# A graph network's first two stages share one SBUF buffer, and the loop that sums edges is written out on two engines

## The chip, the cores and the metric

The kernel runs on one core of one Trainium2 chip. A core has five engines that work at the same time and meet through semaphores: TensorE (PE, matrix products into PSUM), VectorE (DVE), ScalarE (ACT), GpSimd (POOL) and SyncE (SP), which issues most transfers. The metric is device microseconds of one execution, the median of several runs. Everything is float32.

## The reference, cut to what matters

1250 nodes have 512 features each, and 40000 edges (`src`, `dst`, `edge_weight`) join them. The change touches the first half of this:

```python
deg = jnp.maximum(segment_sum(ones, dst), 1.0)
xn  = layernorm(x)
x   = x + gnn0(xn, src, dst, deg) + flow_attention(xn)   # gnn0: segment_sum(xn[src], dst)/deg @ W_neigh + xn @ W_self, normed
x   = x + experts0(layernorm(x))
xn  = layernorm(x)
x   = x + gnn1(xn, src, dst, edge_weight) + attention1(xn)   # gnn1 sums with edge weights
x   = x + experts1(layernorm(x))
```

Both sums over edges are products with a dense matrix: `counts[s, d]`, the number of edges from s to d, and `weights[s, d]`, the sum of their weights. The kernel builds both matrices once.

## The kernel before, in words

`program` runs five stages one after the other; a barrier of all engines stands between two of them.

**`flow_attention`** (0 to 600 us of the profile). The 1250 rows lie as `T` = 10 tiles of 125 rows by 512 features. In its first part the 40000 edges get places in a list that is sorted by groups of 32 destinations (`BUCKET`), and POOL writes the edge records to `sorted_edges` in HBM with 320 indirect DMAs (L310), one after the other. Beside that, PE, DVE and ACT compute the attention. DVE ends with `add_up` (L654), which adds the result to x in `g.x`. What is left then are the last tiles of `side(t)`: PE multiplies `xn` with the first graph layer's two matrices (L781, L784), ACT copies both products to a buffer that holds two tiles (L692), and SP stores them in HBM as `neighbour` and `own` (L512). ACT may overwrite its half of the buffer only when the stores of two tiles earlier have landed. After tile 6 SP also stores `g.x` itself as `x_spill` (L515), since its SBUF place is given up at the end of the stage.

**`adjacency`** (601 to 921 us) builds `counts` and `weights`, each 10 blocks of 1280 columns on 128 partitions, in a large buffer called `arena`. DVE first sets `counts` to zero (L923), POOL `weights` (L894). The sorted list has `NG` = 118 groups of 512 edges (4 chunks of 128). For each group:
- DVE makes 4 one-hot matrices of 128x320 of the destinations (L931) and the one-hot rows (128x128) of chunk 3 of the sources (L933);
- POOL copies three columns of numbers (L901) and makes the one-hot rows of chunks 0 to 2 (L909), then, one group behind, `row_low` of chunk 3 (L914);
- ACT scales the rows by both halves of the weight, 7 operations (L964, L966);
- PE multiplies: 4 matmuls into `ps_c`, 8 into `ps_w` (L982 to L987), at full width 320;
- DVE, two groups behind, adds `ps_c` to the 10x32 columns of `counts` and `ps_w` to those of `weights` (L944). Which 32 columns is read from a table on chip into a register.

All five engines run this as loops over registers, four groups a turn (`staggered`), with 4 buffers (`BUFS`). So group t can begin when the product of group t-4 is done (semaphore `used`).

**`nodes`** (921 us on) reads `x_spill` back into `x_rows` (L1162), sums degrees, and combines. On DVE the sum of a tile is made in `h`, which holds `own` (loaded in the stage before, L889); POOL adds a row of biases to x (L1206). The last two stages are the experts and the gathering of their results.

## Time and profile before

| | us |
|---|---|
| median of 3 runs | 2133.72 |
| lowest and highest of them | 2128.21, 2137.45 |
| the profiled execution | 2126.98 |
| its span, first to last instruction | 2125.2 |
| adjacency: first one-hot of DVE to last addition of a product | 614.34 to 918.76 |

The page of the profile gives each engine's busy time over the whole span: PE 81%, DVE 43%, ACT 24%, POOL 41%. These are means over stages that differ; within `adjacency` all four are busy for most of the time. The rows further down are in us from the span's start. In a row of the timeline the first number is the start and the second the time from there to the end of the last instruction that it merges; the time from one start to the next is the step that the engine needs. "idle before <-" names what ended an engine's idle time.

### The profile page before, as it was taken

How to read it: one execution, taken by the hardware profiler on the slowest of the kernel's cores; microseconds unless marked ns; L12 is line 12 of the kernel's file. 1: busy time of each engine (PE TensorE's matmuls, PEld its weight loads, DVE VectorE, ACT ScalarE, POOL GpSimd, SP SyncE). 2: the span in 40 equal slices, each digit the busy share in tenths (PEclk: the TensorE clock that was granted, in tenths of full speed). 3: DMA queues.
4: the chain of work that ended last, by engine and by line, in shares of the span. 5: the costliest groups of instructions: out<-in, count | busy, mean ns of one | idle time of the engine just before them, and what ended most of it. 6: DMA issues, size and time to landing. Idle time of an engine off the chain costs nothing. (4 is left out here: it accounts for less than half of the span.)

```text
span 2125.2 us, 27922 instructions
## 1 busy us (share of the span) xinstructions
PE 1715.3 (81%) x8075; PEld 1126.1 (53%) x8076; DVE 919.6 (43%) x2223; ACT 519.3 (24%) x1459; POOL 875.1 (41%) x1032
## 2 busy tenths in 40 slices
PE   4649988756937777786879999279999999999992
PEld 4224434334436666652434465157777777777770
DVE  3852266344159999969845638400000000000001
ACT  0011101111138888820111122011222211122220
POOL 0677778777669999965011100220000000043002
PEclk9999998978969999998889999589999999999996
DMA  7900031000230000010210013543803320420003
GB/s 202 298 2 2 2 76 31 2 2 2 65 114 25 0 0 0 0 61 0 94 56 1 0 37 122 211 131 150 331 20 144 150 76 20 178 63 20 20 20 102
DMA packets 77073, 150.32 MB, mean 71 GB/s; under 512 B 19795, under 2 KB 21402, under 8 KB 72802
## 3 DMA queue, kind: packets, MB, share of 16 engines
q1 hardware_dynamic: 50533, 125.26, 16.5%
q0 software_dynamic: 19200, 11.30, 3.7%
q10 hardware_dynamic: 7294, 13.21, 1.8%
q8 instruction: 23, 0.38, 0.1%
q14 instruction: 23, 0.18, 0.0%
HBM read 111.35 MB, written 37.99 MB: 70 GB/s over the span
## 5 line engine op out<-in xcount | busy, mean ns | idle before, releaser
L310 POOL DMA_INDIRECT sorted_edges<-fa_records,fa_edge_slot x320 | 399.4, 1248 | 176.2 <-issue 176.2
L1838 PEld LDWEIGHTS et_ps_h<-et_turned,arena 128*128 128x128 f32 x3072 | 348.6, 193 | 19.2 <-issue 15.9
L1838 PE MATMUL et_ps_h<-et_turned,arena 128*128 128x128 f32 x3072 | 349.1, 276 | 7.6 <-issue 4.5
L1847 PE MATMUL et_ps_y<-arena,et_hidden_t 128*128 x768 | 333.6, 592 | 0.0
L909 POOL TENSOR_SCALAR ad_row<-iota,ad_row_no 128x128 fp32r<-128x128 f32 x354 | 237.9, 685 | 0.1
L1847 PEld LDWEIGHTS et_ps_y<-arena,et_hidden_t 128*128 128x128 f32 x768 | 144.0, 190 | 172.2 <-issue 172.2
L1749 POOL DMA_INDIRECT xn_rows<-slot_out,slots x10 | 12.2, 1218 | 493.8 <-POOLq L1746 491.0
L986 PE MATMUL ad_ps_w<-ad_to,ad_row_high 128*128 128x320 f32 x472 | 150.1, 330 | 63.5 <-POOL ad_row_low L914 60.5
L964 ACT ACTIVATE ad_row_high<-ad_row,ad_edges 128x128 fp32r<-128x128 f32 x472 | 184.5, 391 | 67.9 <-DVE ad_row L933 67.0
L1765 DVE COPY et_turned<-et_ps_t 128x512 f32<-128x512 f32 x25 | 17.3, 692 | 370.7 <-PE et_ps_t L1819 370.7
L931 DVE TENSOR_SCALAR ad_to<-iota,ad_edges 128x320 fp32r<-128x320 f32 x472 | 176.6, 433 | 0.0
L1775 DVE TENSOR_TENSOR et_y<-et_ps_y,et_b 128x512 f32<-128x512 f32 x24 | 16.6, 691 | 318.1 <-PE et_ps_y L1847 318.1
L1795 ACT ACTIVATE et_hidden_t<-et_ps_h,ex_b 128x128 f32<-128x128 f32 x384 | 109.7, 369 | 143.9 <-PE et_ps_h L1838 141.2
L987 PE MATMUL ad_ps_w<-ad_to,ad_row_low 128*128 128x320 f32 x472 | 140.9, 310 | 0.0
L986 PEld LDWEIGHTS ad_ps_w<-ad_to,ad_row_high 128*128 128x128 f32 x472 | 89.4, 189 | 90.9 <-ACT ad_row_high L964 90.9
L966 ACT ACTIVATE ad_row_low<-ad_row,ad_edges 128x128 fp32r<-128x128 f32 x354 | 137.3, 388 | 0.0
L1795 ACT ACT_TABLE_LOAD x24 | 30.8, 1283 | 434.2 <-PE et_ps_h L1838 434.2
L1604 PE MATMUL no_banks<-arena,no_turned 128*125 128x512 f32 (+1 forms) x320 | 114.4, 515 | 7.1 <-ACT no_turned L1231 7.1
L1537 PE MATMUL no_banks<-xn_rows,arena 125*125 125x512 f32 x200 | 97.6, 648 | 21.3 <-DVE arena L1320 17.6
L982 PE MATMUL ad_ps_c<-ad_to,ad_row 128*128 128x320 f32 x472 | 89.6, 312 | 31.3 <-DVE ad_row L933 31.3
L739 PE MATMUL fa_banks<-ident,fa_work 125*128 125x125 f32 x120 | 23.3, 329 | 103.1 <-DVE fa_work L551 45.3
L1216 POOL TENSOR_TENSOR x_rows<-x_rows,no_normed 125x512 f32<-125x512 f32 x10 | 12.7, 1271 | 208.4 <-DVE no_normed L1379 208.4
(363 smaller groups left out, 2327.2 us busy)
## 6 DMA issues: line engine op xcount, KB each, us to landing
arena<-L_ffn_W SPq DMA_DIRECT2D x16, 4096.0 KB, 13.3
slot_rows<-fa_zeros SPq DMA_DIRECT2D x1, 7424.0 KB
slot_out<-fa_zeros SPq DMA_DIRECT2D x1, 6912.0 KB
et_rows_in<-slot_rows ACTq DMA_DIRECT2D x26, 256.0 KB, 2.6
slot_out<-et_y ACTq DMA_DIRECT2D x24, 256.0 KB, 2.0
sorted_edges<-fa_records,fa_edge_slot POOLq DMA_INDIRECT x320
x_in<-x SPq DMA_DIRECT2D x1, 2500.0 KB
neighbour<-fa_Wv SPq DMA_DIRECT2D x10, 250.0 KB
```

Of the source, the lines that this page charges most:

```text
L310: nc.gpsimd.indirect_dma_start(g.sorted_edges, bass.IndirectOffsetOnAxis(ap=self.edge_slot[0:NT, e:e + 1], axis=0), self.records[0:NT, e, ...
L909: last = nc.gpsimd.tensor_scalar(row[:, u, c, :], g.iota[:, 0:P], row_no[:, u, c:c + 1], None, ALU.is_equal)
L931: v.tensor_scalar(to[:, u, c, :], g.iota[:], field(t, c, 1), None, ALU.is_equal)
L964: last = nc.scalar.activation(row_high[:, u, c, :], row[:, u, c, :].bitcast(F32), ACT.Copy, scale=field(t, c, 2))
L966: nc.scalar.activation(row_low[:, u, c, :], row[:, u, c, :].bitcast(F32), ACT.Copy, scale=field(t, c, 3))
L986: pe.matmul(ps_w[:, u, 0:ONE_HOT], row_high[:, u, c, :], to[:, u, c, :], start=(c == 0), stop=False)
L987: last = pe.matmul(ps_w[:, u, 0:ONE_HOT], row_low[:, u, c, :], to[:, u, c, :], start=False, stop=(c == CHUNKS - 1))
L1537: last = pe.matmul(banks[r, t % 3, :], counts[r, b, t * NT:(t + 1) * NT], g.xn[r, b, :], start=(b == 0), stop=(b == T - 1))
L1604: last = pe.matmul(banks[r, bank, 0:GCN] if name == "conv" else banks[r, bank, :], turned[:, t % 2, k * NT:(k + 1) * NT], matrix[:, k, :], ...
L1795: last = nc.scalar.activation(hidden_t[:, f * KD + i, :], ps_h[:, f % 2, i, :], ACT.Gelu, bias=x.b1[:, bass.ds(e * FT + (f * KD + i), 1)])
L1838: last = pe.matmul(ps_h[:, f % 2, i, :], x.weights[:, at:at + P], turned[:, k, :], start=(k == 0), stop=(k == KD - 1))
L1847: last = pe.matmul(ps_y[:], hidden_t[:, i, :], x.weights[:, bass.ds(buffer * (2 * HALF) + (HALF + i * D), D)], start=(i == 0), stop=(i == ...
```

## The change

It does five things.

1. **x stays on chip.** `arena` (32768 float32 a partition) is made at the very start. `g.x` in the first stage is its part behind `weights` and `counts`, which now lie side by side at its front. The first stage's big buffers (q, k, v, work, Wo, W1, W2 and others) are cut out of that front. `x_spill`, its store and its load are gone.
2. **The zeroing moves.** DVE clears both matrices (25600 elements a partition) in one memset at the end of the first stage, behind `add_up`. Both memsets of `adjacency` are gone.
3. **`own`** is loaded at the start of `nodes` into `x_rows`, where `x_spill` was loaded, and not during `adjacency`. In `nodes` the buffers `h` and `g.x` change their roles.
4. **The loops of DVE and POOL are written out** for all 118 groups, so that addresses are constants; only the columns of the addition stay in a register. ACT and PE keep their loops. POOL's copy of the numbers is gone. POOL makes 3 rows in even groups and 2 in odd ones; DVE makes 1 and 2. POOL's `row_low` runs two groups behind, where it ran one behind.
5. **One addition a group**: `ps_w` and `ps_c` are halves of one PSUM tensor, and one DVE instruction adds 2x10x32 columns to both matrices.

```diff
-                if t == SIDE[1]:
-                    sp.wait_ge(s["x_final"], 1)
-                    sp.dma_start(g.x_spill.rearrange("(t p) d -> p t d", p=NT), g.x[0:NT]).then_inc(s["x_stored"], 16)
-            sp.wait_ge(s["x_stored"], 16)
...
             staggered(c, 8, prepare_ff, nothing, add_up)
             c.settle()
-            dve.sem_inc(s["x_final"], 1)
+            c.link(v.memset(arena[:, 0:2 * T * DST], 0.0))
...
-        ps_c, ps_w = m.psum("ps_c", [P, BUFS, 512]), m.psum("ps_w", [P, BUFS, 512])
+        ps = m.psum("ps", [P, BUFS, 2, 512])
+        ps_w, ps_c = ps[:, :, 0, :], ps[:, :, 1, :]
+        totals = arena[:, 0:2 * T * DST].rearrange("p (m b n) -> p m b n", m=2, b=T)
...
+        def pool_rows(t):
+            return 3 - t % 2
...
-            sp.dma_start(own_rows[0:NT], g.own.rearrange("(t p) d -> p t d", p=NT)).then_inc(arrived, 16)
...
-            nc.gpsimd.memset(weights, 0.0).then_inc(zeroed, 1)
...
-                for c in range(POOL_ROWS):
-                    last = nc.gpsimd.tensor_scalar(row[:, u, c, :], g.iota[:, 0:P], row_no[:, u, c:c + 1], None, ALU.is_equal)
+                for c in range(pool_rows(t)):
+                    last = nc.gpsimd.tensor_scalar(row[:, u, c, :], g.iota[:, 0:P], field(t, c, 0), None, ALU.is_equal)
...
-            staggered(Steps(pool, chain), 0, fetch_numbers, build_rows, scale_low, NG, BUFS)
+            in_turn(build_rows, scale_low, NG, BUFS)
...
-                for ps, total in ((ps_c, counts), (ps_w, weights)):
-                    part = total[:, :, bass.ds(at, BUCKET)]
-                    last = v.tensor_tensor(part, part, ps[:, u, 0:ONE_HOT].rearrange("p (b n) -> p b n", b=T), ALU.add)
+                part = totals[:, :, :, bass.ds(at, BUCKET)]
+                v.tensor_tensor(part, part, ps[:, u, :, 0:ONE_HOT].rearrange("p m (b n) -> p m b n", b=T), ALU.add).then_inc(added, 1)
...
-            sp.dma_start(g.x[0:NT], g.x_spill.rearrange("(t p) d -> p t d", p=NT)).then_inc(s["x_in"], 16)
+            sp.dma_start(g.x[0:NT], g.own.rearrange("(t p) d -> p t d", p=NT)).then_inc(s["own_in"], 16)
```

`in_turn(first, third, n, ways)` is a plain loop that calls `first(t)` and then `third(t - 2)`, for t from 0 to n + 1.

What that does to an engine's row of instructions is seen at three places. On DVE, the end of one group in the middle of `adjacency` (ISA and REGISTER_ALU rows compute addresses in registers, and one ISA row stands ahead of each of the four one-hots) before:

```order
L931 TENSOR_SCALAR ad_to<-iota,ad_edges 128x320
L933 ISA
L933 TENSOR_SCALAR ad_row<-iota,ad_edges 128x128
L937 ISA
L937 TENSOR_LOAD group_offset
L937 ISA x2
L939 REGISTER_ALU
L941 REGISTER_ALU [waits ad_used]
L944 ISA [waits ad_added]
L944 TENSOR_TENSOR arena<-arena,ad_ps_c 128x10x32
L944 ISA
L944 TENSOR_TENSOR arena<-arena,ad_ps_w 128x10x32
```

And a whole group of DVE at the same place after the change, an odd one:

```order
L947 TENSOR_SCALAR ad_to<-iota,ad_edges 128x320 [waits ad_used]
L947 TENSOR_SCALAR ad_to<-iota,ad_edges 128x320 x3
L949 TENSOR_SCALAR ad_row<-iota,ad_edges 128x128 x2
L953 TENSOR_LOAD group_offset
L953 ISA x2
L959 ISA [waits ad_added,ad_used]
L959 TENSOR_TENSOR arena<-arena,ad_ps 128x20x32
```

The address steps between the one-hots are gone, the two additions are one of twice the size, and every second group has a second row. On POOL, one group in the same place before:

```order
L901 COPY ad_row_no<-ad_edges 128x3
L909 TENSOR_SCALAR ad_row<-iota,ad_row_no 128x128 [waits ad_used,ad_numbered]
L909 TENSOR_SCALAR ad_row<-iota,ad_row_no 128x128 x2
L914 ISA [waits ad_columns_made]
L914 TENSOR_TENSOR ad_row_low<-ad_row,ad_edges 128x128
```

And two groups of POOL after the change:

```order
L929 TENSOR_SCALAR ad_row<-iota,ad_edges 128x128 [waits ad_used]
L929 TENSOR_SCALAR ad_row<-iota,ad_edges 128x128 x2
L934 TENSOR_TENSOR ad_row_low<-ad_row,ad_edges 128x128 [waits ad_columns_made]
L929 TENSOR_SCALAR ad_row<-iota,ad_edges 128x128 [waits ad_used]
L929 TENSOR_SCALAR ad_row<-iota,ad_edges 128x128
L934 TENSOR_TENSOR ad_row_low<-ad_row,ad_edges 128x128 [waits ad_columns_made]
```

The copy is gone, and five rows stand where six stood. On DVE at the passage from the first stage to `adjacency`, before:

```order
L654 TENSOR_TENSOR x_in<-x_in,fa_work 125x512 [waits fa_f_out]
L448 UNCONDITIONAL_BRANCH [waits fa_chain]
L920 UNCONDITIONAL_BRANCH [waits barrier_Pool_Activation_PE_DVE_SP_release]
L923 MEMSET arena 128x12800
L931 TENSOR_SCALAR ad_to<-iota,ad_edges 128x320 [waits ad_loaded,ad_used,ad_zeroed,ad_chain]
```

And the same passage after:

```order
L680 TENSOR_TENSOR arena<-arena 125x512 [waits fa_f_out]
L684 MEMSET arena 128x25600 [waits fa_chain]
L474 UNCONDITIONAL_BRANCH [waits fa_chain]
L939 UNCONDITIONAL_BRANCH [waits barrier_Pool_Activation_PE_DVE_SP_release]
L947 TENSOR_SCALAR ad_to<-iota,ad_edges 128x320 [waits ad_used,ad_loaded]
```

The memset has moved to the other side of the barrier and doubled.

## Rows read from the trace of the kernel before

**Rows 1.** Busy time by stretch: engines with counts, granted clock, DMA share, GB/s

```profile
614.30:921.40 307.10, 237.95 (x1417) 210.32 (x1417) 302.18 (x838) 254.92 (x826) 299.91 (x585) 0.98 0.04 14
```

**Rows 2.** Timeline, end of the first stage: start, us, engine, line, instruction [idle before]

```profile
546.58 0.69 DVE L654 TENSOR_TENSOR x_in<-x_in,fa_work 125x512 f32<-125x512 f32 x1
...
555.97 0.34 SPq L515 DMA_DIRECT2D x_spill<-x_in  x1
...
577.65 7.75 SPq L512 DMA_DIRECT2D own<-fa_Wv  x1
...
579.26 1.19 POOL L310 DMA_INDIRECT sorted_edges<-fa_records,fa_edge_slot  x1 [0.30 <-issue]
...
583.87 1.12 PE L784 MATMUL fa_banks<-fa_bq,ones 1*125 1x512 f32 x2
592.38 1.07 ACT L692 COPY fa_Wv<-fa_banks 125x512 f32<-125x512 f32 x2 [17.32 <-DMA own<-fa_Wv]
...
593.48 0.25 SPq L512 DMA_DIRECT2D own<-fa_Wv  x1
```

**Rows 3.** Timeline, start of adjacency, SP and DVE

```profile
600.85 0.35 SPq L886 DMA_DIRECT2D ad_edges<-sorted_edges  x1
...
603.58 10.72 DVE L923 MEMSET arena<- 128x12800 f32 x1 [56.32 <-issue]
605.45 0.27 SPq L888 DMA_DIRECT2D xn_rows<-neighbour  x1
...
614.34 1.57 DVE L931 TENSOR_SCALAR ad_to<-iota,ad_edges 128x320 fp32r<-128x320 f32 x4
```

**Rows 4.** Timeline of DVE near the program's start, POOL idle

```profile
11.54 0.33 DVE L327 MEMSET fa_turned<- 128x320 f32 x1
11.88 0.33 DVE L328 MEMSET fa_turned<- 40x320 f32 x1
...
12.30 0.31 DVE L331 CAST fa_high_r<-fa_work 125x320 fp32r<-125x320 f32 x1
12.53 0.32 DVE L332 CAST fa_turned<-fa_work 125x320 f32<-125x320 int32 x1
...
13.41 0.76 DVE L335 TENSOR_TENSOR fa_records<-fa_work,fa_high_r 125x320 f32<-125x320 f32 x1
```

**Rows 5.** Timeline, one group in the loop's steady part: DVE, POOL and ACT

```profile
903.89 2.01 POOL L909 TENSOR_SCALAR ad_row<-iota,ad_row_no 128x128 fp32r<-128x128 f32 x3
...
904.57 1.50 DVE L931 TENSOR_SCALAR ad_to<-iota,ad_edges 128x320 fp32r<-128x320 f32 x4
...
905.87 0.46 POOL L914 TENSOR_TENSOR ad_row_low<-ad_row,ad_edges 128x128 fp32r<-128x128 f32 x1
...
905.99 0.41 DVE L933 TENSOR_SCALAR ad_row<-iota,ad_edges 128x128 fp32r<-128x128 f32 x1
...
906.33 0.47 DVE L944 TENSOR_TENSOR arena<-arena,ad_ps_c 128x320 f32 x1
...
906.43 2.01 POOL L909 TENSOR_SCALAR ad_row<-iota,ad_row_no 128x128 fp32r<-128x128 f32 x3
...
906.50 0.40 ACT L964 ACTIVATE ad_row_high<-ad_row,ad_edges 128x128 fp32r<-128x128 f32 x1 [0.28 <-DVE ad_row L933]
...
906.72 0.47 DVE L944 TENSOR_TENSOR arena<-arena,ad_ps_w 128x320 f32 x1
```

**Rows 6.** Timeline of DVE where the groups already have constant addresses: first and last

```profile
617.61 0.30 DVE L933 TENSOR_SCALAR ad_row<-iota,ad_edges 128x128 fp32r<-128x128 f32 x1
617.81 1.43 DVE L931 TENSOR_SCALAR ad_to<-iota,ad_edges 128x320 fp32r<-128x320 f32 x4
...
912.22 1.42 DVE L931 TENSOR_SCALAR ad_to<-iota,ad_edges 128x320 fp32r<-128x320 f32 x4
913.57 0.41 DVE L933 TENSOR_SCALAR ad_row<-iota,ad_edges 128x128 fp32r<-128x128 f32 x1
```

**Rows 7.** Timeline, start of nodes, POOL

```profile
946.73 13.18 POOL L1206 TENSOR_TENSOR x_rows<-x_rows,arena 125x512 f32<-125x512 f32 x10 [10.40 <-DMA no_gate_b<-L_ffn_bg]
```

More of the change, by code:

```diff
@@ L123, in staggered, with in_turn @@
     third(n - 1, (n - 1) % ways)
+def in_turn(first, third, n, ways):
+    for t in range(n + 2):
+        if t < n:
+            first(t, t % ways)
+        if t >= 2:
+            third(t - 2, (t - 2) % ways)
 def nothing(t, u):
@@ L853, in _, with adjacency @@
                 side(t)
-def adjacency(nc, g, counts, weights, own_rows):
+def adjacency(nc, g, arena):
     BUFS = 4
-    POOL_ROWS = 3
     POOL_LOW = 1
@@ L922, in _ @@
             v = nc.vector
-            v.memset(counts, 0.0).then_inc(chain, 1)
-            dve.wait_ge(chain, 1)
-            dve.wait_ge(zeroed, 1)
             dve.wait_ge(loaded, 16)
@@ L931, in build_columns @@
                     v.tensor_scalar(to[:, u, c, :], g.iota[:], field(t, c, 1), None, ALU.is_equal)
-                for c in range(POOL_ROWS, CHUNKS):
+                for c in range(pool_rows(t), CHUNKS):
                     last = v.tensor_scalar(row[:, u, c, :], g.iota[:, 0:P], field(t, c, 0), None, ALU.is_equal)
@@ L941, in add @@
                 dve.wait_ge(added, t + BUFS)
-                for ps, total in ((ps_c, counts), (ps_w, weights)):
-                    part = total[:, :, bass.ds(at, BUCKET)]
-                    last = v.tensor_tensor(part, part, ps[:, u, 0:ONE_HOT].rearrange("p (b n) -> p b n", b=T), ALU.add)
-                last.then_inc(added, 1)
-            staggered(Steps(dve, chain), 0, build_columns, nothing, add, NG, BUFS)
+                part = totals[:, :, :, bass.ds(at, BUCKET)]
+                v.tensor_tensor(part, part, ps[:, u, :, 0:ONE_HOT].rearrange("p m (b n) -> p m b n", b=T), ALU.add).then_inc(added, 1)
+            in_turn(build_columns, add, NG, BUFS)
             dve.wait_ge(added, NG + BUFS)
@@ L953, in _ @@
             last.then_inc(chain, 1)
-            dve.wait_ge(chain, 2)
+            dve.wait_ge(chain, 1)
         @block.scalar
@@ L1885, in program @@
         g = Shared(nc, stack)
-        with ExitStack() as first:
-            g.x = Memory(nc, first).sb("x_in", [P, T, D])
-            flow_attention(nc, A, g)
+        arena = Memory(nc, stack).sb("arena", [P, 2 * 2 * HALF])
+        weights, counts = (arena[:, i * T * DST:(i + 1) * T * DST].rearrange("p (t n) -> p t n", t=T) for i in range(2))
+        rows = arena[:, 2 * T * DST:2 * T * DST + T * D].rearrange("p (t d) -> p t d", t=T)
+        g.x = rows
+        flow_attention(nc, A, g, arena)
         with ExitStack() as layer:
-            arena = Memory(nc, layer).sb("arena", [P, 2 * 2 * HALF])
             x = Experts(nc, A, layer, arena)
-            weights, counts = (arena[:, i:i + T * DST].rearrange("p (t n) -> p t n", t=T) for i in (0, T * DST + T * D))
-            h = arena[:, T * DST:T * DST + T * D].rearrange("p (t d) -> p t d", t=T)
-            adjacency(nc, g, counts, weights, h)
+            adjacency(nc, g, arena)
             g.x = Memory(nc, layer).sb("x_rows", [P, T, D])
-            nodes(nc, A, g, x, arena, weights, counts, h)
+            nodes(nc, A, g, x, arena, weights, counts, rows)
             expert_tiles(nc, A, g, x)
```

72 lines of the change are left out of this document (40 added, 32 removed).

## The prediction

> **What bounds the kernel now.** I read the busy time by stretch first, then the timeline of the two places that the diff touches. In `adjacency` (307.10 us) DVE is busy for 302.18 us and POOL for 299.91, ACT for 254.92, PE for 237.95, and PE's granted clock is 0.98, the level of 2.4 GHz [rows 1]. So two engines have no slack there. The steady part shows it: POOL starts its three rows at 903.89 and again at 906.43, so a group takes 2.54 us; DVE's one-hots start at 904.57, its row at 905.99, its additions at 906.33 and 906.72, each right behind the one before, while ACT waits 0.28 us for DVE's row [rows 5]. 118 groups at 2.55 are 301 of the 304.4 us between first one-hot and last addition.
>
> At the passage into `adjacency` other things end last. PE's last product of the first stage ends at 584.99 (583.87 + 1.12). ACT copies it only from 592.38, after 17.32 us of idle time that a store of `own` ended; that store stood in SP's queue behind the 2.5 MB of `x_spill`, issued at 555.97, and its issue alone took 7.75 us [rows 2]. The last store goes out at 593.48 [rows 2], and the edge list is asked for at 600.85, behind the barrier [rows 3]. It is there at 605.45, where SP goes on, but DVE makes its first one-hot at 614.34, since its memset comes first [rows 3].
>
> **The change part by part.**
>
> *x is not stored.* Without the spill the stores of tile 7 go out when they are made, and ACT's wait goes. Next late is PE's last product, at 584.99, then a copy of 0.6, so the last store goes out at about 585.7, which is 7.8 earlier than 593.48. Before, it had a second store 0.5 us ahead of it, and both and the barrier took 7.4 us (593.48 to 600.85). After, that other store is over 4 us ahead. So 7.4 is the upper bound and 4.7, somewhat over half, the lower; I take 5.2, nearer the lower, as only one store is left to wait for. The edge list is then asked for at 590.9, 10 us earlier (bounds 7.8 and 10.5). POOL's last indirect DMA was issued at 579.26 [rows 2]; nothing makes it later, and 11 us are left for it to land.
>
> *The memset moves.* DVE's memset of 320 elements takes 0.335 us from start to start (11.54 to 11.88) [rows 4], 1.04 ns an element. 12800 elements are 13.4 us: DVE was free from the barrier at about 600.9 and went on at 614.3, so the row's 10.72 shows only its later part [rows 3]. 25600 elements take 26.8 us. DVE's last addition ends at 547.3 [rows 2], so it is done at 574.1, covered by the stage's end at 590, with 16 us to spare. If that cover were gone it would cost what lies over 590. In `adjacency` DVE then waits for the edge list alone: 614.34 - 605.45 = 8.9 us less, sure within 0.3.
>
> The Trainium skill (SBUF — State Buffer, "SBUF: two separate sides") warns that VectorE work which takes both ports keeps GpSimd from writing the descriptors of its DMAs, and POOL still has such DMAs to issue when the new memset runs. The same skill (VectorE: DVE Perf Modes, "Zero memsets can be issued as uint32") gives a memset one cycle an element, and the 1.04 ns above agree, so I take it for no such work; the other case is a rival.
>
> *`own` is loaded later.* It takes the place of the load of `x_spill`, of the same 2.5 MB, as first transfer of `nodes`. POOL's wait there was ended by the small `gate_b` behind it in the queue [rows 7], and that stays. DVE needs both too. 0 us.
>
> *The loop, for one group.* DVE is the engine to sum, in steps from start to start:
> - four one-hots: 1.42 in the loop (904.57 to 905.99) [rows 5], 1.35 with constant addresses (912.22 to 913.57) [rows 6]: -0.07.
> - half a row more: 0.20 where another comparison follows (617.61 to 617.81) [rows 6], 0.34 ahead of an addition [rows 5]: +0.10, at worst +0.17.
> - the additions: 0.39 and 0.40 before (906.33 to 906.72, and on to the next group). The second now lacks its start and costs its elements alone, 320 at 1.04 ns [rows 4]: 0.40 + 0.33 = 0.73, so -0.06. Bounds: 0 if nothing is saved; the slow form is a rival.
> - what DVE and POOL cost each other. A one-hot takes 0.34 while POOL works; a cast of the same 320 elements takes 0.23 with POOL idle (12.30 to 12.53) [rows 4]. With the row (0.34 against 0.20) that is 4 x 0.11 + 0.14 = 0.58 us a group that POOL's presence costs. POOL was busy for 98% [rows 1]. After, it makes 2.5 rows at 0.66 (three took 903.89 to 905.87) and one `row_low` of 0.46 [rows 5], 2.1 us of 2.4: idle for a seventh. A seventh of 0.58 is 0.08; were all of the 0.3 us idle under one-hots, it would be 0.3 x 0.58 / 1.69 = 0.10. I take -0.09. The bounds are 0 and -0.58.
>
> Sum: -0.12 us, 2.43 a group; times 118, 14 us. ACT's 254.92 / 118 = 2.16 us a group [rows 1] lies below that and PE's 2.02 too, so both keep their slack. POOL's copy was free of DVE and goes with it. `row_low` is a group later: it follows the rows of group t+2, which follow the product of t-2, and two groups at 2.43 are 4.86 us against about 2.0 + 0.5 for POOL and 1.3 for the product. It hides. That code written out comes slower to an engine is not seen in any row; 0.
>
> **Sum**: 10 + 8.9 + 14 = 33 us. The profiled execution took 2126.98 us, below the lowest of the three runs, so its own figure would be 2094; against the median of 2133.72 it is 2101, which I forecast.
>
> **The rivals.**
>
> *POOL's slack frees DVE altogether.* If the 0.58 us go for the most part, ACT's loop becomes the bound at 2.16 a group: (2.55 - 2.16) x 118 = 46, and 2133.7 - 19 - 46 = 2069. For it speaks that both engines run in lock-step now, without a gap; against it that POOL stays busy for over four fifths. The Trainium skill (SBUF — State Buffer, "Who interferes with whom") says that the two engines' shared ports are an exclusive lock, held for a whole instruction, and the loser fully blocks. By that rule half a row of 0.6 and the copy of 0.18 would come off the shared time, 0.48 us a group or 57 in all, near 2058. The rows disagree so far: DVE makes four one-hots and a row from 904.57 to 906.33 while POOL makes three rows from 903.89 to 905.87 [rows 5]; in turn they would need more than 2.54 us.
>
> *Nothing comes off the loop.* POOL's idle time falls under DVE's additions, where it helps nobody, and the extra half row eats the rest: 2.50 to 2.58 a group, and 2133.7 - 19 with -6 to +4: 2109 to 2119.
>
> *The memset stops POOL's DMAs*, the skill's warning. Then 26.8 us are added to POOL's chain, 580.5 + 26.8 = 607 and a landing, some 10 us behind 600.85 and not 10 ahead of it: 2101 + 20 = 2121. Against it: 1.04 ns an element.
>
> *The wide addition is slow*, the one that ends slower. An addition with strided operands took 0.76 us for 320 elements, at 13.41 [rows 4], where L944 takes 0.47 [rows 5]. Should 2x10x32 columns fall to that, it takes 1.5 us, not 0.73: +0.79 a group, +93 us, near 2194. From a step of 1.10 us on the kernel gets slower than before by 0.5%. Against it: the parts before had the same runs of 32 and did not pay for them.
>
> **How the numbers follow.** Forecast (2092 to 2109) 0.50; POOL's slack frees DVE (2058 to 2092) 0.25; nothing off the loop 0.15; memset stops POOL 0.05; slow addition 0.05. A measurement of this kernel can tell about 0.5%, 10.7 us, from no change. Below 2123 lie the first three and most of the fourth: faster 0.90, same 0.05, slower 0.05. The range runs from 2066, which leaves out a part of the second case, to 2119.
>
> **What would show it.** The edge list asked for near 591 and the first one-hot 4.6 us behind it; no wait of ACT on `own`; the memset between 547 and 574, POOL's 1.5 us rhythm of indirect DMAs unbroken beside it. In the loop: period near 2.43; the addition's step 0.73; one-hots 0.31 to 0.34; ACT waiting for DVE about 0.2 us a group, POOL idle for 0.3. A period of 2.16 with ACT never idle is the first rival, one-hots still at 0.34 with POOL idle the second. I am wrong altogether if the addition's step is over 1.1 us or POOL's DMAs stop from 547 on.

## The result, and the profile after

The changed kernel takes 2096.31 us (median of 4 runs, 2095.41 to 2099.82), the kernel before 2130.97 in the same comparison (4 runs, 2123.45 to 2137.45). The ratio is 0.984, with a 95% interval of 0.981 to 0.988. The forecast was 2101, 4.7 us above, with a range of 2066 to 2119. The profiled execution took 2099.82 us (span 2098.0), the one of before 2126.98.

First the busy times of the changed kernel by stretch: the first stage up to VectorE's last addition, the passage up to the first one-hot, the edge sum, and the rest in three. The columns after the stretch are its length and each engine's busy us.

```profile
core 0: us, PE busy (x) PEld busy (x) DVE busy (x) ACT busy (x) POOL busy (x), PEclk, DMA share, GB/s
0.00:544.90 544.90, 382.69 (x1353) 198.70 (x1355) 268.33 (x475) 56.87 (x104) 378.72 (x312) 0.94 0.26 60
544.90:593.10 48.20, 35.72 (x84) 14.36 (x82) 21.43 (x2) 6.39 (x11) 25.23 (x22) 0.87 0.27 65
593.10:887.30 294.20, 241.11 (x1416) 210.27 (x1416) 287.90 (x767) 254.57 (x826) 257.15 (x413) 0.98 0.02 9
887.30:1036.80 149.50, 116.58 (x364) 57.26 (x364) 119.45 (x313) 14.64 (x22) 53.59 (x28) 0.87 0.16 55
1036.80:1387.40 350.60, 272.02 (x1056) 159.71 (x1057) 179.60 (x551) 50.88 (x103) 52.32 (x40) 0.87 0.22 79
1387.40:2098.00 710.60, 668.40 (x3805) 484.38 (x3803) 40.70 (x58) 135.56 (x395) 52.81 (x40) 0.97 0.28 99
```

The stretches of before were 547.3, 67.0, 304.5, 148.9, 346.8 and 710.7 us long. Side by side, with the last three put together:

| stretch | before | after | difference |
|---|---|---|---|
| first stage | 547.3 | 544.9 | -2.4 |
| VectorE's last addition there to first one-hot | 67.1 | 48.2 | -18.9 |
| first one-hot to end of last edge addition | 304.4 | 294.3 | -10.1 |
| from there to the end | 1206.4 | 1210.6 | +4.2 |

The change shows in the second and third line, 29.0 us together. The other two lines hold its quieter parts (x in `arena`, `own` loaded in `nodes`), and they differ between executions of one kernel too. From the last addition to the end of TensorE's last product in `nodes` it is 433.5 us before, 434.9 in this profile, 436.7 in a second profile of the changed kernel (after_again) and 433.5 in store_x, a variant that loads `own` at the same place: that load costs nothing that can be seen. The whole part behind the edge sum takes 1207.3 to 1214.5 us in the profiles of the changed kernel and its variants and 1206.4 in the single one of before. Whether a few us of that are a cost of the change is not shown.

The passage, in the changed kernel's timeline of VectorE, SyncE's queue and ScalarE (start, duration, what runs, idle time before it and its releaser):

```profile
544.21 0.69 DVE L680 TENSOR_TENSOR arena<-arena 125x512 f32<-125x512 f32 x1
550.29 21.39 DVE L684 MEMSET arena<- 128x25600 f32 x1 [5.40 <-issue]
...
582.65 0.59 ACT L718 COPY fa_Wv<-fa_banks 125x512 f32<-125x512 f32 x1 [3.84 <-PE fa_banks L810]
...
583.26 0.25 SPq L542 DMA_DIRECT2D own<-fa_Wv  x1
587.62 0.35 SPq L916 DMA_DIRECT2D ad_edges<-sorted_edges  x1
```

ScalarE's last copy waits for its product only, where the one of before waited 17.32 us for a store of `own` [rows 2]. The edge list is asked for 42.7 us after VectorE's last addition; before it was 53.6 (600.85 less 547.27) [rows 3]. From asking to the first one-hot it is 5.4 us, where it was 13.5. These two steps are 10.9 and 8.0 us.

The start of the loop, on GpSimd, TensorE and VectorE:

```profile
593.12 5.81 POOL L929 TENSOR_SCALAR ad_row<-iota,ad_edges 128x128 fp32r<-128x128 f32 x8 [13.21 <-DMA ad_edges<-sorted_edges]
598.90 0.40 POOL L934 TENSOR_TENSOR ad_row_low<-ad_row,ad_edges 128x128 fp32r<-128x128 f32 x1
...
599.45 0.61 PE L1000 MATMUL ad_ps<-ad_to,ad_row_high 128*128 128x320 f32 x1 [2.36 <-POOL ad_row_low L934]
...
593.06 1.52 DVE L947 TENSOR_SCALAR ad_to<-iota,ad_edges 128x320 fp32r<-128x320 f32 x4 [21.37 <-DMA ad_edges<-sorted_edges]
...
602.07 0.82 DVE L959 TENSOR_TENSOR arena<-arena,ad_ps 128x640 f32 x1 [3.87 <-PE ad_ps L1001]
```

The first addition comes 9.0 us after the first one-hot; before it was 6.85. TensorE waits 2.36 us for `row_low` of group 0, which stands behind eight rows on GpSimd. No term of the prediction had this.

The steady part, VectorE, then GpSimd, then ScalarE:

```profile
751.37 0.81 DVE L959 TENSOR_TENSOR arena<-arena,ad_ps 128x640 f32 x1
752.10 1.36 DVE L947 TENSOR_SCALAR ad_to<-iota,ad_edges 128x320 fp32r<-128x320 f32 x4
753.39 0.30 DVE L949 TENSOR_SCALAR ad_row<-iota,ad_edges 128x128 fp32r<-128x128 f32 x1
753.58 0.81 DVE L959 TENSOR_TENSOR arena<-arena,ad_ps 128x640 f32 x1
...
751.96 0.40 POOL L934 TENSOR_TENSOR ad_row_low<-ad_row,ad_edges 128x128 fp32r<-128x128 f32 x1
752.72 2.14 POOL L929 TENSOR_SCALAR ad_row<-iota,ad_edges 128x128 fp32r<-128x128 f32 x3 [0.35 <-PE ad_ps L1001]
754.82 0.46 POOL L934 TENSOR_TENSOR ad_row_low<-ad_row,ad_edges 128x128 fp32r<-128x128 f32 x1
...
751.70 0.40 ACT L978 ACTIVATE ad_row_high<-ad_row,ad_edges 128x128 fp32r<-128x128 f32 x1 [0.57 <-DVE ad_row L949]
```

VectorE runs without a gap: the addition's step is 0.73 us (751.37 to 752.10), a group with one row on VectorE takes 2.21. The next one, with two, takes about 2.65. The 21st addition starts at 650.95 and the 111th at 870.57, 2.440 us a group; before these were 671.68 and 901.22, 2.550. GpSimd now waits 0.35 us for the product; it had no idle time in [rows 5].

### The profile page after: what moved, and what is told of

Read it like the earlier page. It is cut to its first block and busy times, and to the rows that moved or that the text cites. A ratio compares the mean times of both kernels' runs of the same rounds, so it can differ in the third digit from the quotient of the medians.

```text
span 2098.0 us, 26207 instructions
## 1 busy us (share of the span) xinstructions
PE 1716.5 (82%) x8075; PEld 1124.7 (54%) x8076; DVE 917.4 (44%) x2164; ACT 518.9 (25%) x1459; POOL 819.8 (39%) x854
## 5 line engine op out<-in xcount | busy, mean ns | idle before, releaser
L929 POOL TENSOR_SCALAR ad_row<-iota,ad_edges 128x128 fp32r<-128x128 f32 x295 | 210.8, 727 | 42.8 <-PE ad_ps L1001 29.6
L1000 PE MATMUL ad_ps<-ad_to,ad_row_high 128*128 128x320 f32 x472 | 153.2, 337 | 49.6 <-ACT ad_row_high L978 46.8
L947 DVE TENSOR_SCALAR ad_to<-iota,ad_edges 128x320 fp32r<-128x320 f32 x472 | 168.3, 415 | 21.4 <-DMA ad_edges<-sorted_edges 21.4
L1001 PE MATMUL ad_ps<-ad_to,ad_row_low 128*128 128x320 f32 x472 | 140.9, 310 | 0.0
L1000 PEld LDWEIGHTS ad_ps<-ad_to,ad_row_high 128*128 128x128 f32 x472 | 89.4, 189 | 80.2 <-ACT ad_row_high L978 77.5
L765 PE MATMUL fa_banks<-ident,arena 125*128 125x125 f32 x120 | 22.6, 321 | 102.9 <-DVE arena L577 45.4
L996 PE MATMUL ad_ps<-ad_to,ad_row 128*128 128x320 f32 x472 | 89.6, 312 | 13.1 <-POOL ad_row L929 13.1
L959 DVE TENSOR_TENSOR arena<-arena,ad_ps 128x640 f32 x118 | 95.3, 807 | 6.3 <-PE ad_ps L1001 6.2
```

What stands on the lines that cost most here:

```text
L929: last = nc.gpsimd.tensor_scalar(row[:, u, c, :], g.iota[:, 0:P], field(t, c, 0), None, ALU.is_equal)
L947: v.tensor_scalar(to[:, u, c, :], g.iota[:], field(t, c, 1), None, ALU.is_equal)
L959: v.tensor_tensor(part, part, ps[:, u, :, 0:ONE_HOT].rearrange("p m (b n) -> p m b n", b=T), ALU.add).then_inc(added, 1)
L1000: pe.matmul(ps_w[:, u, 0:ONE_HOT], row_high[:, u, c, :], to[:, u, c, :], start=(c == 0), stop=False)
L1001: last = pe.matmul(ps_w[:, u, 0:ONE_HOT], row_low[:, u, c, :], to[:, u, c, :], start=False, stop=(c == CHUNKS - 1))
```

## The experiments

All are the changed kernel with the edit named; after_again has none. The table has the numbers of each profile on which the verdicts rest: **passage** is from VectorE's last addition of the first stage to the first one-hot, **start** from there to the first edge addition, **period** from the 21st to the 111th addition divided by 90, **sum** from the first one-hot to the end of the last addition, all in us. The median is of all its timed executions; pool_idle, whose results are wrong, has a single one.

| kernel | passage | start | period | sum | median |
|---|---|---|---|---|---|
| before | 67.1 | 6.85 | 2.550 | 304.4 | 2130.97 |
| changed kernel | 48.2 | 9.0 | 2.440 | 294.3 | 2096.31 |
| after_again | 48.2 | 9.0 | 2.431 | 293.3 | 2094.87 |
| store_x | 57.9 | 9.0 | 2.429 | 293.6 | 2112.74 |
| clear_in_adjacency | 56.2 | 6.9 | 2.429 | 291.4 | 2107.81 |
| low_early | 46.4 | 7.4 | 2.431 | 291.7 | 2093.13 |
| two_adds | 48.0 | 9.0 | 2.418 | 292.2 | 2094.09 |
| dve_rolled | 48.2 | 9.0 | 2.425 | 293.0 | 2095.81 |
| pool3 | 49.3 | 9.6 | 2.410 | 291.3 | 2091.94 |
| pool_idle | 48.3 | 9.0 | 2.218 | 269.3 | 2076.14 |
| dve_as_before | 48.1 | 9.6 | 2.486 | 300.4 | 2105.39 |
| pool_as_before | 47.9 | 8.1 | 2.617 | 314.0 | 2115.19 |
| best | 47.9 | 7.7 | 2.392 | 287.6 | 2091.28 |
| best2 | 48.0 | 7.7 | 2.419 | 291.0 | 2098.88 |

The kernel before, timed beside the later ones, had medians of 2124.6 to 2126.3. The medians carry some us that no edit explains, so sizes of single edits are read from the stretches of each kernel's one profile.

**The measure.**

> The changed kernel itself once more, as the measure for the other runs beside it: period of a group 2.43 to 2.44, first addition 9.0 us after the first one-hot, 294 us from the first one-hot to the end of the last addition, 48 us from VectorE's last addition of the first stage to the first one-hot. What differs between its profile and the first one (outside adjacency above all) is what one profiled execution can't tell.

It held. The period differs by 0.009 and the sum by 1.0 us from the first profile, in which three groups took 0.22 us longer than their like. The part behind the edge sum took 1209.2 us, 1.4 less than in the first profile. How far one passage can be trusted is seen in low_early and pool3, which edit nothing there: 46.4 and 49.3 us. From asking for the edge list to the first one-hot it is 5.2 to 5.5 us in every run that leaves it alone.

### The passage

**The store of x, put back.**

> The changed kernel, with x stored to the spill buffer again between the stores of neighbour and own, and waited for at the end of the stage (nothing reads it). Theory: the store of own queues behind it and ScalarE's last copies wait, so the edge list is asked for 10 to 11 us later, 53 to 54 us after VectorE's last addition of the first stage where it was 42.7; adjacency itself unchanged; the total 10 to 11 us more. Rival: in the kernel before the delay came from GpSimd's scatter or the barrier, and the store costs under 5 us. The clear of the totals, now at the same time, is not touched.

```
+                if t == SIDE[1]:
+                    sp.wait_ge(s["x_final"], 1)
+                    sp.dma_start(g.x_spill..., g.x[0:NT]).then_inc(s["x_stored"], 16)
+            sp.wait_ge(s["x_stored"], 16)
```

SyncE's queue and ScalarE of this kernel:

```profile
550.79 0.36 SPq L546 DMA_DIRECT2D x_spill<-arena  x1
555.50 13.12 SPq L543 DMA_DIRECT2D neighbour<-fa_Wv  x1
...
587.37 0.25 SPq L543 DMA_DIRECT2D own<-fa_Wv  x1
594.81 0.35 SPq L922 DMA_DIRECT2D ad_edges<-sorted_edges  x1
...
586.27 1.07 ACT L724 COPY fa_Wv<-fa_banks 125x512 f32<-125x512 f32 x2 [16.38 <-DMA own<-fa_Wv]
```

The pattern of before is back: an issue that takes 13.12 us behind the big store, ScalarE 16.38 us without work until a store of `own` has landed. The edge list is asked for 52.7 us after the first stage's last addition (594.81 less 542.10) and not 42.7. The cost is 9.8 us in the passage and nothing elsewhere; the rival (under 5 us) falls. Of the delay, 3.1 us lie behind the last store: 7.44 us from it to the asking, against 4.36 without the big store in the queue.

**The clear, put back into adjacency.**

> The changed kernel, with the totals cleared where the kernel before did it: at the start of adjacency, half by VectorE and half by GpSimd. Theory: from the asking for the edge list to the first one-hot 13.5 us instead of 5.44, so 8.05 later. GpSimd's half ends about 2 us before VectorE's, so GpSimd gets a lead and the first addition comes 7 to 7.5 us after the first one-hot instead of 9.01: 6 us more in all up to the last addition. Rival 1: no lead, 8 us more. Rival 2: the clear beside the first stage was not free and its removal there gives something back (GpSimd's last indirect DMA or the last store of own earlier by over 1 us): under 5 us more.

```
-            c.link(v.memset(arena[:, 0:2 * T * DST], 0.0))
+            nc.gpsimd.memset(arena[:, 0:T * DST], 0.0).then_inc(zeroed, 1)      # GpSimd, adjacency
+            v.memset(arena[:, T * DST:2 * T * DST], 0.0).then_inc(chain, 1)     # VectorE, adjacency
```

Timeline of SyncE, VectorE and GpSimd:

```profile
592.53 0.35 SPq L915 DMA_DIRECT2D ad_edges<-sorted_edges  x1
...
595.27 10.72 DVE L942 MEMSET arena<- 128x12800 f32 x1 [45.46 <-issue]
606.03 1.62 DVE L950 TENSOR_SCALAR ad_to<-iota,ad_edges 128x320 fp32r<-128x320 f32 x4
...
592.98 10.76 POOL L922 MEMSET arena<- 128x12800 f32 x1 [13.17 <-POOLq L474]
603.73 5.11 POOL L929 TENSOR_SCALAR ad_row<-iota,ad_edges 128x128 fp32r<-128x128 f32 x8
```

From asking to the first one-hot it is 13.50 us, as forecast. GpSimd starts 2.3 us ahead of VectorE, and the start takes 6.9 us instead of 9.0. So the clear costs 8.1 us and gives back 2.1 at the start, with `row_low` as late as in the changed kernel; passage and sum together are 5.1 us longer than in the first profile of the changed kernel and 6.1 longer than in the second. That is the theory (6 us, by way of the lead); 8 falls, and so does a gain of over 3 us elsewhere. GpSimd's last indirect DMA starts 28.8 us after the first stage's last addition (578.63 less 549.81), against 33.8 and 30.3 in the two profiles of the changed kernel, but the edge list waits for the last store of `own` (588.17), not for it.

**What the medians say of these two.** store_x is 17.9 us slower than after_again, clear_in_adjacency 12.9: 8 and 7 us more than in the stretches. TensorE's mean granted clock goes with it: 0.938 to 0.942 in the four executions of after_again, 0.934 to 0.938 in the six of store_x, 0.933 to 0.939 in the four of clear_in_adjacency. Executions of one kernel differ like that too: of the nine of the kernel before that were timed beside after_again, one took 2136.11 us at 0.933, one 2123.26 at 0.938 and one 2120.39 at 0.936. So a lower clock goes with a longer time, but not strictly; that it makes these 7 to 8 us is likely and not shown, and why these two kernels are granted less is open. The granted clock in the passage, 0.79 before and 0.87 after, is part of the mean and too little of it: by an estimate from these figures, 10 us more at 0.79 move the mean over 2100 us by 0.001.

**row_low earlier.**

> The changed kernel, with GpSimd's row_low of a group made one group after its rows instead of two (as in the kernel before). Start theory: the changed kernel loses about 2 us at the start of adjacency, because row_low of group 0 stands behind eight rows on GpSimd and the first addition comes 9.01 us after the first one-hot, where it was 6.85. With the shorter lag it stands behind five rows: the first addition 6.8 to 7.2 us after the first one-hot, the steady period 2.43 as before, the total 2 us less. Rival: the lag matters in the steady part, GpSimd waits for VectorE's row in every group, and the period rises to 2.48 or more, the total by 4 us or more. Second rival: what ends the start is TensorE or ScalarE, the first addition stays at 9.0.

```
-            in_turn(build_rows, scale_low, NG, BUFS)
+            in_turn(build_rows, scale_low, NG, BUFS, 1)     # third(t - 1), not third(t - 2)
```

Start of the loop on GpSimd, TensorE and VectorE:

```profile
588.88 3.86 POOL L929 TENSOR_SCALAR ad_row<-iota,ad_edges 128x128 fp32r<-128x128 f32 x5 [11.71 <-DMA ad_edges<-sorted_edges]
592.71 0.46 POOL L934 TENSOR_TENSOR ad_row_low<-ad_row,ad_edges 128x128 fp32r<-128x128 f32 x1
...
593.59 0.63 PE L1000 MATMUL ad_ps<-ad_to,ad_row_high 128*128 128x320 f32 x1 [0.74 <-ACT ad_row_high L978]
...
596.23 0.82 DVE L959 TENSOR_TENSOR arena<-arena,ad_ps 128x640 f32 x1 [2.25 <-PE ad_ps L1001]
```

`row_low` now follows five rows, TensorE waits for ScalarE and not for it, and the start is 7.4 us. The start theory holds in kind (1.6 us of the 2.2 that were lost, a little less than the 1.8 to 2.2 expected). It isn't the only cause: the start is 6.9 us in clear_in_adjacency, where `row_low` stayed late and GpSimd had its lead back. So the 2.2 us are lost where the later `row_low` and the lost lead come together; in the steady part the lag changes nothing, 2.431 in both.

### The loop

**Two additions again.**

> The changed kernel, with two additions of 128x320 a group instead of one of 128x640. Theory of the prediction, VectorE's steps add up: the additions take 0.79 to 0.82 a group instead of 0.73 to 0.71, the period goes from 2.43 to 2.49 to 2.53, 7 to 12 us more. Rival, VectorE's step is covered by the wait for the product or given back by GpSimd's free time: period 2.43 to 2.45, up to 2 us more.

```
-                part = totals[:, :, :, bass.ds(at, BUCKET)]
-                v.tensor_tensor(part, part, ps[:, u, :, 0:ONE_HOT]..., ALU.add).then_inc(added, 1)
+                for m_ in (1, 0):
+                    part = totals[:, m_, :, bass.ds(at, BUCKET)]
+                    last = v.tensor_tensor(part, part, ps[:, u, m_, 0:ONE_HOT]..., ALU.add)
```

The two take 0.79 us a group (752.50 to 753.29) instead of 0.73, as the prediction priced them, and yet the period falls from 2.431 to 2.418. Groups of instructions of this kernel in the edge sum (busy us, mean ns of one, idle time before):

```profile
L947 DVE TENSOR_SCALAR ad_to<-iota,ad_edges 128x320 fp32r<-128x320 f32 x472 | 161.4, 401 | 21.2 <-DMA ad_edges<-sorted_edges 21.2
...
L960 DVE TENSOR_TENSOR arena<-arena,ad_ps 128x320 f32 x236 | 103.0, 475 | 6.1 <-PE ad_ps L1003 6.1
```

A one-hot's row has a mean of 401 ns here and 415 in the changed kernel, so four of them give back about 0.06 us. The theory (2.49 to 2.53) falls. The period even lies a little under the rival's 2.43 to 2.45: the wide addition is worth nothing in this loop.

**VectorE's addresses in registers again.**

> The changed kernel, with VectorE's work in adjacency in a loop with register addresses again, four groups a round; GpSimd's stays written out, the split of the rows and the wide addition stay. Theory of the prediction: a one-hot through a register costs 0.07 a group more (1.42 against 1.35 for four), the period goes from 2.43 to 2.50, 8 us more. Rival: what made the one-hots shorter is GpSimd's freer time and not the addresses, the period stays within 0.01 of 2.43. Second rival: with GpSimd less loaded the loop's own branch and register work shows, 2.55 or more.

```
-            in_turn(build_columns, add, NG, BUFS)
+            staggered(Steps(dve, chain), 0, build_columns, nothing, add, NG, BUFS)
```

The period is 2.425, the one-hots' mean 412 ns. The first rival holds in its number: the constant addresses on VectorE are worth nothing here. The shorter one-hots of [rows 6], on which the prediction rested this term, lie in the last group. GpSimd was busy beside them, but without its copy of the row numbers; its rows in the kernel before:

```profile
908.82 0.18 POOL L901 COPY ad_row_no<-ad_edges 128x3 f32<-128x3 f32 x1
...
910.96 0.46 POOL L914 TENSOR_TENSOR ad_row_low<-ad_row,ad_edges 128x128 fp32r<-128x128 f32 x1
911.40 2.06 POOL L909 TENSOR_SCALAR ad_row<-iota,ad_row_no 128x128 fp32r<-128x128 f32 x3
```

The one-hots of 912.22 to 913.57 fall under the last three rows (911.40 to 913.46) and the `row_low` behind them. In pool3, next, which has three rows and no copy on GpSimd throughout, four one-hots take 1.35 us as well (751.62 to 752.96).

**Three rows on GpSimd.**

> The changed kernel, with GpSimd making three rows in every group (as in the kernel before) and VectorE one. Theory A, both engines limit: GpSimd needs three rows of about 0.66 us and a row_low of 0.46 without its copy, a period of 2.36 to 2.40, 4 to 8 us less than the changed kernel. Theory B, VectorE alone limits and GpSimd has room: its groups with one row take 2.21 already, so the period is 2.21 and the time 25 us less. Theory C, the split was worth its place, GpSimd and VectorE slow each other more with GpSimd always busy: the period is 2.43 to 2.48 and nothing is won or some us are lost.

The edit is `return 3` for `return 3 - t % 2`. Period 2.410: theory A, just above its range of 2.36 to 2.40, and B and C fall. Both engines run without a gap (of 280.8 us from the first addition to the last, VectorE is busy 278.5 and GpSimd 275.6). The half row that the change moved to VectorE, together with GpSimd's relief, costs 0.02 a group; the start is 0.6 us longer with three rows a group, which leaves 2.0 us less in the sum.

**GpSimd nearly without work.**

> The changed kernel, with GpSimd's operations on rows and row_low cut to 2 of 128 columns from the fifth group on (so the weights and counts of these groups are wrong); number and order of all instructions and waits stay. Theory: GpSimd's presence costs VectorE time. Its one-hots go to 0.295 and its rows to 0.2, a group to 2.11 with one row and 2.31 with two, 2.21 on the mean, unless ScalarE or TensorE take over at 2.16: period 2.16 to 2.25, 21 to 32 us less. Rival: VectorE's steps don't depend on GpSimd, period 2.40 to 2.44.

```
-                    last = nc.gpsimd.tensor_scalar(row[:, u, c, :], g.iota[:, 0:P], ...)
+                    n = P if t < BUFS else 2
+                    last = nc.gpsimd.tensor_scalar(row[:, u, c, 0:n], g.iota[:, 0:n], ...)
```

VectorE's timeline, and under it its groups in the edge sum:

```profile
750.97 0.81 DVE L961 TENSOR_TENSOR arena<-arena,ad_ps 128x640 f32 x1
751.70 1.27 DVE L949 TENSOR_SCALAR ad_to<-iota,ad_edges 128x320 fp32r<-128x320 f32 x4
752.89 0.50 DVE L951 TENSOR_SCALAR ad_row<-iota,ad_edges 128x128 fp32r<-128x128 f32 x2
753.29 0.81 DVE L961 TENSOR_TENSOR arena<-arena,ad_ps 128x640 f32 x1
```

```profile
L949 DVE TENSOR_SCALAR ad_to<-iota,ad_edges 128x320 fp32r<-128x320 f32 x472 | 149.7, 375 | 21.5 <-DMA ad_edges<-sorted_edges 21.5
...
L961 DVE TENSOR_TENSOR arena<-arena,ad_ps 128x640 f32 x118 | 95.3, 807 | 6.4 <-PE ad_ps L1003 6.4
```

The theory holds. GpSimd is still busy for 124.8 of 269.3 us, so VectorE is not quite alone. Four one-hots take 1.19 us (751.70 to 752.89), a group 2.11 with one row and 2.32 with two. So of 2.43 in the changed kernel 2.22 are VectorE's own and 0.21 come from GpSimd's presence. The addition is 807 ns here and 807 in the changed kernel, where a one-hot is 375 here and 415 there: GpSimd slows the one-hots and leaves the addition alone.

So three parts of the loop's change are worth nothing each, or next to it, when undone alone. That leaves GpSimd's code: the copy of the row numbers is gone and its loop is written out. The next two kernels put each side of the loop as it was.

**VectorE's side as before.**

> The changed kernel, with VectorE's part of the loop as in the kernel before (a loop with register addresses, one row a group, two additions of 128x320) and GpSimd's written out with constant addresses, three rows a group and no copy. Theory, formed after the first eight runs: the period of 2.55 was GpSimd's own (copy, three rows, row_low), and what the change brought in the loop is the copy that is gone; VectorE's changes are worth nothing, because a shorter step of VectorE only moves its one-hots under more of GpSimd's work. Then the period is 2.40 to 2.43 here. Rival: VectorE's changes count when all three are undone at once (0.07 for addresses, 0.10 for the addition), 2.48 to 2.55.

Period 2.486, with 0.79 for the additions. The theory falls and the rival holds, at the low end of its range. GpSimd's new code, with three rows still, brings 0.064 of the 0.11 to 0.12 (2.550 to 2.486). How much of that is the copy, and how much the written-out loop, no run separates. VectorE's register addresses and two additions together cost 0.076 against pool3, although beside two and a half rows on GpSimd each alone costs nothing. The edge sum fits: 300.4 us.

**GpSimd's side as before.**

> The changed kernel, with GpSimd's part of the loop as in the kernel before (a loop, a copy of three row numbers for each group, three rows, row_low one group after the rows) and VectorE's written out with constant addresses, one row a group and the wide addition. Theory: GpSimd alone sets the period, 2.53 to 2.57 as in the kernel before, although VectorE has everything that the change gave it. Rival: VectorE's shorter additions count, 2.43 to 2.48. The first addition comes 7.5 to 8.5 us after the first one-hot, since row_low is early again.

Timeline of VectorE and GpSimd, and under it the group of the one-hots:

```profile
751.87 0.81 DVE L969 TENSOR_TENSOR arena<-arena,ad_ps 128x640 f32 x1
752.60 1.66 DVE L957 TENSOR_SCALAR ad_to<-iota,ad_edges 128x320 fp32r<-128x320 f32 x4
754.19 0.38 DVE L959 TENSOR_SCALAR ad_row<-iota,ad_edges 128x128 fp32r<-128x128 f32 x1
754.49 0.81 DVE L969 TENSOR_TENSOR arena<-arena,ad_ps 128x640 f32 x1
...
752.66 0.39 POOL L943 TENSOR_TENSOR ad_row_low<-ad_row,ad_edges 128x128 fp32r<-128x128 f32 x1
753.00 0.28 POOL L930 COPY ad_row_no<-ad_edges 128x3 f32 x1
753.26 2.04 POOL L938 TENSOR_SCALAR ad_row<-iota,ad_row_no 128x128 fp32r<-128x128 f32 x3
```

```profile
L957 DVE TENSOR_SCALAR ad_to<-iota,ad_edges 128x320 fp32r<-128x320 f32 x472 | 195.4, 473 | 21.1 <-DMA ad_edges<-sorted_edges 21.1
```

Period 2.617, above both ranges and above the kernel before, which has the same work on GpSimd and more on VectorE. Four one-hots take 1.59 us here (752.60 to 754.19), 1.42 before [rows 5]. With the shorter addition and constant addresses on VectorE the loop is slower by 0.07. That GpSimd alone sets the period is false too: the same GpSimd code runs at 2.55 and at 2.62, without a gap in both. Its instructions themselves take other times: the copy 0.18 before (908.82, above) and 0.28 here (753.00).

### A kernel faster than both

**best.**

> The changed kernel with GpSimd making three rows in every group, row_low of a group one group after its rows, and ScalarE making the fourth row_low in every second group (eight scalings of 0.294 us there instead of seven), so that GpSimd's row_low runs in half the groups. Theory: VectorE alone needs 2.11 a group with one row, GpSimd busy for 2.0 to 2.2 costs it 0.25 to 0.27: period 2.36 to 2.38 where it is 2.43, and the first addition 1.5 to 3 us earlier; 8 to 11 us less than the changed kernel. Rival: ScalarE, 2.36 in the groups with eight scalings and no slack left, becomes the bound, the period is 2.43 or more. Second rival: GpSimd was no longer what slows VectorE, the period stays at 2.41 as with three rows alone.

```
-            return 3 - t % 2
+            return 3
...
+                if t % 2 == 0:
+                    return                       # GpSimd: no row_low in every second group
...
-            in_turn(build_rows, scale_low, NG, BUFS)
+            in_turn(build_rows, scale_low, NG, BUFS, 1)
...
-                    if c < CHUNKS - POOL_LOW:
+                    if c < CHUNKS - POOL_LOW * (u % 2):      # ScalarE: eight scalings there
```

Period 2.392, a little above the theory's 2.36 to 2.38; the sum is 287.6 us, 5.7 less than after_again, and not the 8 to 11 expected. low_early's earlier `row_low` and pool3's rows alone make 1.6 and 2.0 of that. The engines in the edge sum:

```profile
589.70:877.40 287.70, 240.42 (x1416) 209.55 (x1416) 282.19 (x709) 266.31 (x885) 268.51 (x413) 0.99 0.03 9
```

Its ratio to the kernel before is 0.985 (0.983 to 0.987), that of the changed kernel 0.984 and 0.983 in two comparisons. In the stretch the gain is plain; in the whole time, 2091.28 against 2096.31 and 2094.87, it is smaller than the intervals.

**best2.**

> As the run best (row_low one group after the rows; ScalarE makes the fourth row_low in every second group), but GpSimd makes three rows in the groups where ScalarE takes row_low and two in the others, VectorE one and two. VectorE alone needs 2.21 a group on the mean; GpSimd is busy for about 1.65 of it, less than in any run so far. Theory, the less GpSimd does the less VectorE is held up: period 2.30 to 2.36, first addition 7 to 7.5 us after the first one-hot, 281 to 284 us from the first one-hot to the end of the last addition where best took 287.6 and the changed kernel 293.3. Rival: the cost depends on which instruction of one engine lies beside which of the other more than on how much GpSimd does, and the period is anywhere from 2.36 to 2.42. Second rival: ScalarE with eight scalings (2.36) in every second group holds those groups, and the mean is 2.36 or more.

The theory missed: 2.419, although GpSimd is busy for only 226.1 of 291.1 us, less than in best (268.5 of 287.7). The groups alternate between 2.40 and 2.43. The first rival holds by its range, and the second (ScalarE) isn't excluded by this run, since ScalarE is busy for 269.0 of the 291.1 us.

## Why the prediction was right, and where it was not

**The passage was right in mechanism and size.** The store of x: 10 forecast, 10.9 between the two kernels, 9.8 when it alone is put back. The prediction's 5.2 us from the last store to the edge list (bounds 4.7 to 7.4) measured 4.36, a little below its lower bound. The clear: 8.9 forecast, 8.0 measured, 8.1 when put back; the term lost 0.8 because the edge list takes 5.4 us from asking to the first one-hot and not 4.6. Sum 19 against 18.9. The clear ran from behind the last addition (544.90) to its end at 571.68, 26.8 us, inside the time that TensorE's last products take, as forecast. GpSimd's indirect DMAs kept their 1.49 us steps beside it but for one pause of 3.69 us; before, with no clear there, one pause was 6.33. The rival in which the memset stops the DMAs did not occur. The Trainium skill (SBUF — State Buffer, "SBUF: two separate sides") gives its warning for VectorE's two-port modes; with 1.05 ns an element this memset shows no sign of one.

**The loop: 14 forecast, 10.1 measured, and the right period for partly wrong reasons.** The steady period was forecast as 2.43 and is 2.440 and 2.431. What failed:

- *"It hides"*, said of `row_low` one group later. In the steady part it does, in the start it costs: the rows of two more groups lie ahead of it while every other engine waits. The same start had been shortened by GpSimd's lead, which went with its half of the clear, and the prediction had no term for that either. The two together are a missing term of 2.2 us, of which low_early took back 1.6 and clear_in_adjacency 2.1, each alone.
- *One-hots -0.07 by constant addresses.* The size is that of the difference between [rows 5] and [rows 6], but dve_rolled shows that the addresses are worth nothing beside two and a half rows. What else differed at the end of [rows 6] was that GpSimd made no copy. Addresses alone were not undone beside three rows.
- *Additions -0.06.* The step fell as forecast, from 0.79 to 0.73. two_adds shows that this isn't time won: the one-hots get longer by as much.
- *Half a row +0.10.* pool3 gives 0.02 for the whole move of half a row, GpSimd's relief included.
- *VectorE's and GpSimd's mutual cost, -0.09.* It was priced at 0.58 a group from a cast of 0.23 us with GpSimd idle; a one-hot's step is 0.297 in pool_idle. The whole cost measured 0.21 a group in the changed kernel. For the kernel before the steps of pool_idle, with two additions, give an estimate of 2.11 + 0.06 = 2.17 without GpSimd, so 0.38 of its 2.55. The -0.09 itself was measured by no run alone.

The method that failed is the adding up of steps on one engine. That four terms of which two alone are worth nothing add up to the right 0.12 is chance. Undone singly they give 0 (addition), 0 (addresses) and -0.02 (split); undone in groups 0.06 (GpSimd's copy and register loop) and 0.08 (addition and addresses at three rows).

**The rivals.** *GpSimd's slack frees VectorE altogether* did not happen, nor could it: with GpSimd's operations cut to 2 columns the period is 2.218, VectorE's own, and not ScalarE's 2.16. The exclusive lock that the Trainium skill names (SBUF — State Buffer, "Who interferes with whom"), did it hold for the one-hots, would have taken all of a GpSimd instruction from VectorE; GpSimd is busy for 257.15 us of the edge sum, and cutting its operations from 128 columns to 2 took 132.4 us off that (124.8 are left) and 25.0 off the sum (294.3 less 269.3), so these two engines mostly run side by side. *Nothing comes off the loop* (2.50 to 2.58) was wrong by 0.06. *The wide addition is slow* was wrong, 0.73 us a step.

**The total.** The median's difference of 34.7 us and the profiled pair's of 27.2 bracket the 29.0 of the stretches. The second comparison gives 29.7 (2124.59 from nine executions, less 2094.87). So the forecast difference of 33 is nearer to the first median's than its terms deserved: with more executions the change is worth 29 to 30 us, and the forecast was 3 to 4 too high, which is what the loop did not bring. The forecast time of 2101 still came out above the measured one, since it was taken from a median of before, 2133.72, that nine later executions put at 2124.59. Nothing shows where the other 5 us of the first comparison lie. *`own` is loaded later, 0 us* held, by the 433.5 us above.

## What to carry to other kernels

A barrier or a queue that ends late is worth looking at first: two thirds of this gain were one store taken out of a queue and one clear put under other work, and both were priced to a microsecond from a timeline. Where two engines slow each other in a loop, a shorter step on one is not a shorter period; change one thing at a time, then several together, and measure the period, and expect the same edit to gain, to do nothing or to lose by what runs beside it. When a loop is written in another order, price its first pass apart: what hides in the steady part stands bare there.

## What the runs showed of the hardware

GpSimd slows VectorE's one-hots (one input in SBUF, 128x320, with a scalar for each partition) and leaves its additions (one input in PSUM, one in SBUF) alone. The mean of a one-hot is 375 ns with GpSimd's operations cut to 2 columns, 401 to 415 in two_adds, dve_rolled, pool3 and the changed kernel, 430 in best, 433 in the kernel before and 473 in pool_as_before; the wide addition's mean is 807 or 808 ns in the changed kernel, pool_idle, pool3, pool_as_before and best. The page "SBUF — State Buffer" of the Trainium skill, "Who interferes with whom", lets an instruction with one input in SBUF, outside VectorE's two-port modes, run free of GpSimd. The additions agree with that. The one-hots are slowed, and their speed fits a two-port mode: in pool_idle a one-hot's step is 0.297 us for 320 columns and a row's 0.20 for 128, an estimate of 0.51 ns an element, where the memset below takes 1.05. For such a mode the page has the second of the two engines fully blocked until the first is done; neither engine is blocked like that here, as the 25.0 us for 132.4 us of GpSimd's work show.

The slowing goes both ways. At the start of the changed kernel's loop GpSimd makes eight rows, nearly all of them beside VectorE's one-hots, in 5.81 us (593.12), 0.73 us each. While VectorE stands idle before its first addition (3.87 us up to 602.07), the next two take 1.18, 0.59 each:

```profile
599.28 1.18 POOL L929 TENSOR_SCALAR ad_row<-iota,ad_edges 128x128 fp32r<-128x128 f32 x2
```

So in a loop where both engines run without a gap, neither one's steps can be taken as its own.

How much GpSimd costs VectorE doesn't follow from how busy GpSimd is. With VectorE at one row and the wide addition (2.11 a group alone), GpSimd without a gap costs 0.30 with three rows and `row_low` (pool3), and 0.51 with a copy and a loop over registers in addition (pool_as_before). GpSimd is busy for 93% of the edge sum in best and 78% in best2, and best is the faster one (2.392, 2.419). It looks as if the engines settle into a fixed position to each other, since nearly every group of a kernel, or every second one, has the same length to 0.01 us. That this position is the cause is argued and not shown: no run shifted one engine against the other and left the work as it was.

A VectorE memset of 128x25600 elements reads as 21.39 us in its row, with 5.40 us of idle time before it for which the profile names no releaser. Row and idle time together are 26.8 us, 1.05 ns an element; half of it on each engine at once reads 10.72 and 10.76 us in clear_in_adjacency, and VectorE's half takes 13.5 us from the asking for the edge list to the first one-hot.
